# Early-fusion kernel: two of image 2's query projections move ahead of the second attention's first turn, and the second FFN's weights are prepared differently

## The reference

```python
h = h + _L0_attn_ref(_layernorm(h), ...)   # over the 8 images at one position, squared distances
h = h + _L0_ffn_ref(_layernorm(h), ...)    # 8 experts, top 2 in one group, one shared
h = h + _L1_attn_ref(_layernorm(h), ...)   # per image, 16 heads of 16 in 4 key groups
h = h + _L1_ffn_ref(_layernorm(h), ...)    # 8 experts, top 2, and a shared one of double width
```

## Time and profile before

| | |
|---|---|
| median of 3 timed executions | 814.58 us (813.88 to 816.41) |
| the profiled execution, its own time | 820.07 us |
| its span, first to last instruction | 818.2 us |
| mean granted TensorE clock | 0.981 |
| busy: PE, DVE, ACT, POOL | 745.6 (91%), 583.7 (71%), 338.8 (41%), 127.3 us (16%) |
| turn 1, first row scores to turn 2's first scores | 357.80 to 377.32 us |
| six output projections | 579.5 to 595.3 us |
| first experts of the second FFN | 617.6 us |

### The profile page before, as it was taken

One profiled execution on the slowest core, in us unless ns is written; L12 is line 12 of the kernel. 1 busy time (PEld: TensorE's weight loads), 2 busy tenths in 40 slices (PEclk: granted clock), 3 DMA queues, 4 the chain that ended last, 5 costly groups with the idle time before them and its releaser, 6 DMA issues.

```text
span 818.2 us, 13681 instructions
## 1 busy us (share of the span) xinstructions
PE 745.6 (91%) x4993; PEld 610.5 (75%) x4993; DVE 583.7 (71%) x1229; ACT 338.8 (41%) x595; POOL 127.3 (16%) x121
## 2 busy tenths in 40 slices
PE   3279996799999999999999999999998999999997
PEld 3259994699999999865444444444766999999997
DVE  6986767677777777847666666667786677777776
ACT  1214554433333333214777767665433333333332
POOL 0205651000000000070121542222500000000000
PEclk9999996999999999989999999999999999999999
DMA  8500000000000000082345664212200000000000
GB/s 322 208 1 1 0 2 0 1 1 1 1 2 2 0 0 0 2 194 70 81 102 77 118 112 98 41 20 78 127 0 1 1 20 21 1 21 19 2 20 20
DMA packets 21186, 36.54 MB, mean 45 GB/s; under 512 B 6301, under 2 KB 16957, under 8 KB 20489
## 3 DMA queue, kind: packets, MB, share of 16 engines
q1 hardware_dynamic: 16328, 33.12, 15.2%
q10 hardware_dynamic: 4800, 2.66, 2.0%
HBM read 25.79 MB, written 9.95 MB: 44 GB/s over the span
## 4 chain that ended last, share of the span: by engine, by line
PE 83%; DVE 11%; issue 2%; ACT 2%; DMA 2%; POOL 0%; SPq 0%; DVEq 0%; POOLq 0%
PE PS L1248 17%; PE PS L1250 17%; PE PS L1249 17%; PE PS L1507 7%; PE PS L1482 5%; PE PS L1491 5%; PE PS L1515 3%; PE PS L1256 2%; PE PS L1598 2%; DVE MX L1160 2%; PE PS L1331 1%; PE PS L1365 1%; PE PS L1276 1%; DMA x_in<-in_x 1%; PE PS L1565 1%
## 5 line engine op out<-in xcount | busy, mean ns | idle before, releaser
L1160 DVE TENSOR_REDUCE MX<-PS 128x2 f32<-128x576 f32 x144 | 108.7, 756 | 61.8 <-PE PS L1491 61.4
L1086 DVE SCALAR_TENSOR_TENSOR h<-PS,cmb,h 128x256 f32<-128x256 f32 (+1 forms) x342 | 143.9, 476 | 0.2 <-PE PS L1250 0.2
L692 ACT ACTIVATE PR<-PS 96x768 f32<-96x768 f32 x144 | 115.9, 807 | 55.7 <-PE PS L1482 55.2
L633 ACT ACTIVATE sg<-PS 128x384 f32<-128x384 f32 x114 | 56.1, 493 | 164.4 <-PE PS L1250 164.4
L1071 DVE TENSOR_TENSOR al<-aa,ah 128x384 fp32r<-128x384 f32 x114 | 63.6, 558 | 67.1 <-ACT ah L637 67.1
L637 ACT ACTIVATE ah<-aa 128x384 fp32r<-128x384 f32 x114 | 60.0, 526 | 84.0 <-DVE aa L1065 84.0
L1065 DVE TENSOR_TENSOR aa<-sg,PS 128x384 f32<-128x384 f32 x114 | 63.2, 554 | 25.7 <-ACT sg L633 25.2
L1248 PE MATMUL PS<-xTh,W1h 128*128 128x384 f32 x240 | 81.1, 338 | 0.0
L1249 PE MATMUL PS<-xTh,W1l 128*128 128x384 f32 x240 | 80.9, 337 | 0.0
L1250 PE MATMUL PS<-xTl,W1h 128*128 128x384 f32 x240 | 80.8, 337 | 0.0
L1248 PE MATMUL PS<-xTh,W0h 128*128 (+1 forms) x216 | 72.9, 338 | 0.0
(11 more groups left out here) (239 smaller groups left out, 1581.1 us busy)
## 6 DMA issues: line engine op xcount, KB each, us to landing
QS<-scrH SPq DMA_DIRECT2D x28, 144.0 KB, 4.3
W1raw<-in_w SPq DMA_DIRECT2D x1, 3840.0 KB, 12.2
W0raw<-in_w SPq DMA_DIRECT2D x1, 3456.0 KB, 11.3
scrH<-qh SPq DMA_DIRECT2D x8, 432.0 KB, 2.5
scrL<-ql SPq DMA_DIRECT2D x8, 432.0 KB, 2.9
wD<-in_wD SPq DMA_DIRECT2D x1, 2304.0 KB, 11.7
out_tokens<-h SPq DMA_DIRECT2D x6, 384.0 KB, 2.3
x_in<-in_x SPq DMA_DIRECT2D x2, 1024.0 KB, 6.2
```

The costliest lines, as they stand in the source:

```text
L692: A_(PR[0:KT, ca:cb + 1:cb - ca, :], PS[0:KT, b:b + 2, 0:CW], ACT.Exp).then_inc(s["e_exp"], 1)
L1086: ins = V.scalar_tensor_tensor(out=hj, in0=PS[:, b + t // 2, (t % 2) * D:(t % 2) * D + D], scalar=cmb[:, ds(g * GT + t, 1), e:e + 1].squee ...
L1160: V.tensor_reduce(MX[:, hf, z:z + NSH // 2 + 1:NSH // 2], PS[:, b:b + 2, 0:POS], AX_X, ALU.max).then_inc(s["e_mx"], 1)
```

## The change

- `project(2, 0)` and `project(2, 1)` are issued right after those of images 0 and 1, into banks 2 and 3, after a wait for the `query_rows` that read those banks; VectorE's two `query_rows` move likewise. `project(2, 2)` stays at unit 16 of turn 1. ScalarE's and Pool's programs for image 2 keep their places.
- `WARM` goes from 8 to 5, `WARM_P` from 12 to 7. In turn 1 units 0 to 10 have two fillers each; from unit 11 on the number goes by parity as before.
- `NPW` goes from 4 to 6: Pool makes all six low chunks, and VectorE's loop over `low_weights` is empty.
- The weights come in two transfers of half the columns each; ScalarE waits for the first before chunk 0 and for the second before chunk 3.

```diff
--- before.py
+++ after.py
@@ -27,7 +27,7 @@
 GW = GT * P
 REST = NT - GT
 
-NPW = 4
+NPW = 6
 NE = 8
 LN_EPS = 1e-5
 BIG = 3.0e38
@@ -276,7 +276,7 @@
             S[name] = ctx.enter_context(nc.semaphore(name))
         return S[name]
 
-    names = """d_x0 d_x1 t_det t_T t_ev t_acc d_txt d_const d_masks d_wd d_wD d_bias d_qkv d_small d_w0 d_w1 d_a1 d_wo d_out
+    names = """d_x0 d_x1 t_det t_T t_ev t_acc d_txt d_const d_masks d_wd d_wD d_bias d_qkv d_small d_w0 d_w10 d_w11 d_a1 d_wo d_out
         dve_own act_own pool_own var_ready std_ready
         dots_ready dots_sum wex_in wex_ready wts_ready dsc_ready img_done
         const_pool qkv_hi qkv_split rw_split0 rw_split1
@@ -417,7 +417,9 @@
 
         sp.wait_ge(s["e_st"], NU * IMGS)
         sp.wait_ge(s["e_rb"], 16 * 2 * HPG * (IMGS - NLATE))
-        sp.dma_start(W_raw[1][:, :], A["w1"]).then_inc(s["d_w1"], 16)
+        half = sum(WCOLS[1]) // 2
+        for n in range(2):
+            sp.dma_start(W_raw[1][:, n * half:(n + 1) * half], A["w1"][:, n * half:(n + 1) * half]).then_inc(s[f"d_w1{n}"], 16)
         with sp.Fori(0, NG) as g:
             sp.wait_ge(s["f1_acc"], 10 * (g + 1))
             sp.dma_start(out[:, ds(g * GT, GT), :], h[:, ds(g * GT, GT), :]).then_inc(s["d_out"], 16)
@@ -736,8 +738,9 @@
 
         n1 = sum(WCOLS[1]) // NG
         A_(unit[:, :], unit[:, :], ACT.Sqrt)
-        act.wait_ge(s["d_w1"], 16)
         for c in range(NG):
+            if c % (NG // 2) == 0:
+                act.wait_ge(s[f"d_w1{c // (NG // 2)}"], 16)
             z = slice(c * n1, c * n1 + n1)
             A_(W_h[1][:, z], W_raw[1][:, z], ACT.Copy).then_inc(s["w_hi1"], 1)
         std(0, NT)
@@ -1158,7 +1161,7 @@
                         wait(dve, s["e_mT"], 2 * i - 1 + hf)
                     b, z = max_bank(it, c), c % (NSH // 2)
                     V.tensor_reduce(MX[:, hf, z:z + NSH // 2 + 1:NSH // 2], PS[:, b:b + 2, 0:POS], AX_X, ALU.max).then_inc(s["e_mx"], 1)
-                if U in PR_U and live(it, -1) and it > 0:
+                if U in PR_U and live(it, -1) and not early_rows(it + 1, PR_U.index(U)):
                     query_rows(it + 1, PR_U.index(U))
                 for i, b in maxima_at(it, U):
                     dve.wait_ge(s["e_mT"], 2 * i + b + 1)
@@ -1191,7 +1194,7 @@
                         V.tensor_tensor(img(yT[:, g // 2, :], i), a.rearrange("p (j c) -> p j c", j=NT), b.rearrange("p (j c) -> p j c", j=NT), ALU.add)\
                             .then_inc(s["e_yl"], 1)
 
-        for m in range(6):
+        for m in range(8):
             query_rows(m // 3, m % 3)
         for it in range(1, IMGS + 3):
             turn(it)
@@ -1468,7 +1471,9 @@
         def project(i, m):
 
             bank = project_bank(i, m)
-            if i > 1:
+            if i == 2 and early_rows(i, m):
+                pe.wait_ge(s["e_prev"], m + 1)
+            elif i > 1:
                 wait_misc()
                 last[0] = ("e_prev", 3 * i + m + 1)
             split3(PS[:, bank, 0:POS].rearrange("p (j c) -> p j c", j=NT),
@@ -1631,13 +1636,13 @@
 MT_U = [11, 3]
 
 SUM_U, SM_U, REC_U, RO_U, RB_U = [9, 10], 14, 16, 17, list(range(4, 12))
-WARM_P = 12
+WARM_P = 7
 WARM_E = [22, 5, 5, 5, 9]
 S_LEAD = -2
 
 NLATE = 2
 LATE = [(0, 4), (0, 7), (0, 10), (0, 13), (0, 16), (1, 0), (1, 4), (1, 8)]
-WARM = 8
+WARM = 5
 
 Y_G = [0, 2, 1, 3]
 AV_U = [9, 10, 11, 13, 14, 15, 18, 19, 20, 22, 23, 24]
@@ -1656,7 +1661,9 @@
 
 def busy_at(it, U):
 
-    return 1 + U % 2 if it == 1 else 2 if it == 2 and U < AV_U[0] else 0
+    if it == 1:
+        return 2 if U < MT_U[0] else 1 + U % 2
+    return 2 if it == 2 and U < AV_U[0] else 0
 
 
 def av_at(U):
@@ -1718,7 +1725,12 @@
 
 
 def project_bank(i, m):
-    return ((2, 3, 7), (4, 5, 6))[i][m] if i < 2 else 7
+    return ((2, 3, 7), (4, 5, 6))[i][m] if i < 2 else 2 + m if early_rows(i, m) else 7
+
+
+def early_rows(i, m):
+
+    return i < 2 or (i == 2 and m < 2)
 
 
 def live(it, back):
```

## The result

The changed kernel took **826.65 us** in the median of its four timed executions (823.63, 825.92, 827.39, and one of 1728 us that nothing here explains) against 815.5 for four of the kernel before: ratio 1.0116, 95% interval 1.0081 to 1.0152. That is 11 us or 1.4% more, where 809.6 was forecast in a range that ended at 812.6. Without the odd execution the median is 825.92.

The account below looks back on a forecast made before the run. The chain of waits was taken to bound the kernel, TensorE carrying 83% of it. Gains of 2.6 us at the second attention's opening and 2.4 in the last norm, 5.0 together, off 814.58 gave 809.6 us, range 806.8 to 812.6.

Parts of the forecast that it names:

- Part 2: Last norm: without its two low-part subtractions VectorE waits only for ScalarE's root, gaining 2.4 us.
- The port rule: Last norm: Pool locks SBUF ports shared with VectorE; a late Pool could cut the 2.4 us gain to 0.6.
- Part 1 at full clock: Opening of the second attention: turn 1 takes 15.5 us, 4.0 less, if the clock does not fall.
- the maxima's way through DRAM: Image 0's maxima land near 371.6, before turn 2's first `scores` near 373.3: covered by 1.7 us.
- If the timed runs had no fall in turn 1 on either side: Alternative without a clock fall in turn 1: gain of 1.2 there plus 2.4 in the last norm, 811.0 us.
- The step that failed: Turn 1: the clock fall stays but is half as long, 3.4 us, losing 1.4, so the gain is 2.6 us.
- The rival on the slower side: All of turn 1 at the lower clock: 25.2 us, 5.7 more than now; 817.9 us in total, chance 0.05.
- Against: with one or two fillers per unit the clock did come back at 367.0: Argument against the slower outcome: in turn 1 of the old profile the clock returned at 367.0 us.
- The baseline: Whole kernel: the 5.0 us gain was taken off the timed median 814.58, 5.5 below the profiled 820.07.

Follow-up runs that it names:

- e3_warm8: The whole change with 8 warm-up matmuls instead of 5; median 812.67 us, ratio 0.9939 to the kernel before.
- f2_warm7: The whole change with 7 warm-up matmuls instead of 5; median 811.82 us, ratio 0.9960 to the kernel before.
- e1_part2: Only the last norm's part of the change, the opening of the second attention as in the kernel before; median 817.69 us, ratio 0.9993.
- f4_warm8_parity: The whole change with 8 warm-up matmuls instead of 5 and turn 1's fillers by parity as before; median 810.62 us, ratio 0.9922.
- e5_nomove: The whole change, but the two projections stay at units 7 and 12 of turn 1, with 5 warm-up matmuls; median 824.45 us, ratio 1.0089.
- e4_burst: The whole change plus six matmuls of 288 columns at each of units 7 and 12 of turn 1; median 822.02 us, ratio 1.0023.
- f1_before_warm10: The kernel before with 10 warm-up matmuls instead of 8; median 816.71 us, ratio 1.0011.
- g0_whole: The whole change run again unaltered, for its spread; median 823.75 us against 818.21 for the kernel before.
- g2_warm7_three: The whole change with 7 warm-up matmuls instead of 5 and three fillers instead of two at units 3 to 6; median 813.11 us, ratio 0.9948.
- f3_dense: The whole change with five fillers per unit instead of one or two from unit 3 of turn 1 on; median 822.42 us.

## Why the prediction was wrong

- **Part 2 was right.** 2.4 us forecast; 2.6 in the profile (23.4 to 20.8 us from output projection to transposes). The first half of the weights landed 7.2 us after its issue and the second 11.4 after its own (4 us or more apart in the forecast), Pool was through 0.77 us ahead of the moments (0.7 forecast), and VectorE's inversion waited for nothing but the root. The port rule of the Trainium skill ("SBUF — State Buffer", SBUF: two separate sides) was not tested: Pool was done in time, and the moments took 0.17 to 0.19 us each, as before.
- **Part 1 at full clock was right.** 15.5 us forecast, 15.1 measured (`e3_warm8`, `f2_warm7`); the old turn without a fall 16.7 forecast, 16.9 measured (`e1_part2`). The start stayed at 12.8 us behind the first projection, the maxima's way through DRAM did not delay the first `scores`, which waited 0.41 us for VectorE's maximum as before. The one undisturbed execution of the whole change gained 4.3 us; "If the timed runs had no fall in turn 1 on either side" had 3.6; it is one execution.
- **The step that failed** is the clock: "The wait stays and grows, so I keep the fall. I shorten it, because the six units after it now all have two fillers". The wait did grow (from 0.88 to between 1.2 and 1.85 us; "some 1.5" forecast), but it works on the chance of a fall: 53 of 98 executions of the kernel before are not high, 14 of 15 of the whole change. And the fall did not shorten; it lasted 37 to 44 us in the profiles, through turn 1 and well into turn 2, where 3.4 us were forecast. The second filler did not do what I took it to do: the profile after shows the clock at half through nine units of two fillers, and `f4_warm8_parity`, without it, has nine high executions of nine. I also overlooked that the change takes twelve full-height matmuls (weights of 128 rows, where the row scores have 48) of 288 columns out of turn 1, the first six of them from just where the old clock came back (behind the projection of unit 7). That this is why the fall got long fits the profiles, but isn't shown: `e5_nomove`, with both projections in place, is low in five of ten.
- **The rival on the slower side was the right one** and had 0.05: "the lower clock holds through turn 1", priced at 817.9. Turn 1 came out at 24.0 us (25.2 forecast). The price was low for two reasons. It ended with turn 1; the fall goes on for another 21.7 us, and 6.7 us more are lost after turn 1 than before. And it took 25.2 us against the 19.5 of a turn with a fall, but added the difference to a median without one; against the 16.7 of a turn without it is 8.5 us, so 820.7. "Against: with one or two fillers per unit the clock did come back at 367.0" read one execution as a rule.
- **The baseline was mixed.** I took gains worked out against a profile with a fall off a median of three timed executions of which, by their times, none had one (the high ones of before lie at 813.0 to 817.3). The 5.5 us between the profiled execution and the median were in my text as a remark; they were the sign that this kernel has more than one way to run, and that the chance of each is what the change would move.

What stays open: whether the missing projections make a fall long (the place of its end in six profiles speaks for it; the bursts of `e4_burst`, the projection at unit 16 and the five low executions of `e5_nomove` against), whether a shorter wait or more warm-up matmuls prevent it, why the same program falls in one execution and not in the next, and where the three middle executions of `f1_before_warm10` lost their time, as its one profile, of a high execution, shows no fall at the opening.

## What to carry to other kernels

Fillers ahead of a wait can be worth more than they cost even when they compute nothing: count the idle time that TensorE will have left after a move, and cover it to the end. Three warm-up matmuls (1.9 us of TensorE) turned a median 5.5 us above that of before (`g0_whole`) into one 6.6 us below it (`e3_warm8`), each against the kernel before on its own chip. When a profiled execution and the timed median differ by more than the scatter, look for a clock that falls in some executions, forecast both ways of running with a chance each, and take a gain off the baseline that runs the same way. When work moves out of a stretch in which the clock was seen to come back, the old length of the fall is no longer evidence for the new one.

## What the runs showed of the hardware

- Of 98 executions of the kernel before, with 0.88 us of idle time in the one profile, followed by units of row scores (48 of 128 rows) and one or two fillers, 53 did not have a high clock; in that profile it fell to 1.2 GHz. With 2.72 us (`e5_nomove`) none of ten had a high clock. With no wait 42 of 45 had (`e3_warm8`, `f2_warm7`, `g2_warm7_three`, `f4_warm8_parity`), and 9 of 12 of `f1_before_warm10`.
- At 1.2 GHz this mix of instructions ran for 37 to 44 us before the clock came back (four profiles), with TensorE busy without a gap in the records (45.6 of 45.6 us in the windows after); at 2.4 GHz the same mix kept it (1.00 through turn 1 and 21.7 us of turn 2 in `e3_warm8`). With five fillers a unit the lower level lasted 3.5 us (`f3_dense`, one profile).
- The same program, unchanged, had mean clocks from 0.949 to 0.993 and took 813.0 to 837.1 us.
